# One program per engine for three stages, with weight matrices turned between the folds

## The chip, the cores and the metric

One core of a Trainium2 chip runs the whole kernel. The metric is the device time of one execution in microseconds; the runs of the kernel before took 1919.68, 1921.49 and 1924.74 us (median 1921.49). Five engines work at the same time, each on its own list of instructions: TensorE (matmul), VectorE, ScalarE, GpSimd, and SyncE, which here only issues DMAs. They meet only through semaphores, or where a block of the program ends: there all engines wait for all others.

## What is computed

A graph attention over 128 graphs of 128 nodes, 512 features, 16 heads of 32, with only the first 20 nodes of each graph as keys, and two directions of edges:

```python
row_zero = v.sum(-1) == 0
q_exp = where(row_zero[..., None], 0.0, q[:, None, :])
self_feat = concat([v, q_exp], -1) @ W_self.T + b_self
output = self_feat
for d in range(2):
    A = (adj if d == 0 else swapaxes(adj, 1, 2))[:, :, :20, :]
    cond, vb = A.sum(-1), A @ w_bias + b_bias
    kv = self_feat[:, :20]
    qh = (self_feat @ Wq[d].T + bq[d]).reshape(B, N, 16, 32)
    kh = (kv @ Wk[d].T + bk[d]).reshape(B, 20, 16, 32)
    aff = einsum('bnhd,bmhd->bnhm', qh, kh) / sqrt(32)
    w = softmax(where(cond > 0, aff, NEG) + vb, -1)
    output += einsum('bnhf,hgf->bnhg', einsum('bnhm,bmf->bnhf', w, kv), Wout[d]) + bout[d]
return v + relu(output)
```

## The kernel before

There are three stages, and each is a block of its own with one program per engine. Between two blocks all engines meet. Products with weights are made as three products of high and low parts (a number is split into a high part, written by ScalarE, and the rest, written by VectorE or GpSimd).

**Stage one, `prepare_weights`.** TensorE turns weight matrices in 128 x 128 blocks through a ring of six PSUM banks (`turn_bank`); ScalarE and VectorE copy them out. `fold(n)`, eight of them (two directions, four chunks of rows), multiplies the turned Wq with W_self into banks 6 and 7; `fold_high` on ScalarE and `fold_low` on VectorE split the result. `turn_matrix(n)` turns the four matrices Wk[0], Wk[1], Wout[0], Wout[1]; `matrix_high` and `matrix_low` split them, and the low part frees the bank. A small product gives c, the part of self_feat that comes from q (`pe_ct`); four `condition_query(pair)` products give its queries, cq. TensorE's order is: turn W_self, queries 0, folds 0 and 1, queries 1, folds 2 and 3, second half of W_self, q, folds 4 and 5, c, folds 6 and 7, matrices 0 and 1, pairs 0 and 1, matrix 2, pairs 2 and 3, matrix 3, c turned into rows (L447 to L538). The ring's banks go round in that order, pairs included. SyncE loads, and issues the first 80 KB pieces of x (`load_half_rows`, 8 DMAs for a half) after the last fold and after matrix 0; VectorE turns a half (`turn_x`), ScalarE casts it (`x_casts`), GpSimd makes its low part. SyncE ends with waits for the store of c, for all low parts of the matrices and of x.

**Stage two, `keys_and_values`.** Eight halves of 16 graphs. For each half TensorE sums the nodes' features to find zero rows (`sums`, L831), makes the 20 key nodes' features (`features`, L823), and projects them into 8 chunks of keys and 8 of values (`projection`, L823); ScalarE evacuates, VectorE turns values, and SyncE stores both to DRAM: 8 DMAs of keys and 32 of values per half (L616, L622). The last half also turns and splits the first group of x for stage three.

**Stage three, `main_loop`.** 32 groups of four graphs. In the first group: SyncE loads x's own rows xk (L1009), the edges adj0 (one DMA, L1013) and adj1 (four, L1016), waits for all stores and for `cleared`, then loads the next group's rows (L83), keys kbd (L1051) and values vbd (L1063). GpSimd first clears kbd and vbd (L1087, L1088), then makes rc, the conditions' share of each of 8 query chunks (L1116). ScalarE loads the constants wb and bb (L1307, L1308). TensorE makes the zero-row sums (L1462) into bank 4 and then `queries(c)`, c = 0 to 7 (L1482), in two banks; query c waits until query c - 2 has been evacuated by `q_evacuate` on VectorE (L1241). VectorE's order in the first group is: pick of conditions (L1154), nzb (L1234), wait for wb and bb, q_evacuate(0), weigh edges 0 (L1171, waits for adj0), q_evacuate(1), count and total of edges 0, q_evacuate(2), combine, weigh edges 1, q_evacuate(3), and so on.

Of the kernel before, what the change touches and what calls it, by code (L numbers as in the profile page):

```python
# [13 lines left out]
P = 128  # L14
Q = 32
# [75 lines left out]
def build(nc, x, cond, adj, W_self, b_self, w_bias, b_bias, Wq, bq, Wk, bk, Wout, bout, out):  # L91
# [29 lines left out]
    with ExitStack() as whole:  # L121
# [34 lines left out]
        ones = sb("ones", [P, P], F32R)  # L156

        with ExitStack() as keyed:
            sb, _ = scope(keyed)

            wkv_h = sb("wkv_h", [P, 2 * DIRS, C, F], F32R)
            wkv_l = sb("wkv_l", [P, 2 * DIRS, C, F], F32R)
            cb = sb("cb", [P, C, B + 1], F32)
            bk_s = sb("bk_s", [P, DIRS * C], F32)

            with ExitStack() as first:
                prepare_weights(nc, *scope(first), bank, locals())
            with ExitStack() as second:
                keys_and_values(nc, *scope(second), bank, locals())
        with ExitStack() as third:  # L170
            main_loop(nc, *scope(third), bank, locals())


def prepare_weights(nc, sb, sem, bank, v):
# [10 lines left out]
    qt = sb("qt", [P, C, B], F32)  # L185
# [7 lines left out]
    w1 = rows[:, 0:F // Q, :].rearrange("p (j t) k -> p j (t k)", j=R)  # L193
    w2t = nodes_t[:, :, 0:F]
    crows = cond_rows[0:B]
# [26 lines left out]
    wkv_low = sem("wkv_low")  # L222
# [4 lines left out]
    ct_out = sem("ct_out")  # L227
    cq_out = sem("cq_out")
# [3 lines left out]
    bias_done = sem("bias_done")  # L232
    stored = sem("c_stored")
    bk_done = sem("bk_done")
# [14 lines left out]
    M_TURN = [turns(C, lambda j: (wkv_low, j + 1)), turns(C, lambda j: (wkv_low, C + j + 1))]  # L249
    CQ_TURN = list(turns(2, lambda i: (cq_out, 4 * i + 4)))  # L250
    M_TURN.append(turns(C, lambda j: (wkv_low, 2 * C + j + 1)))
    CQ_TURN += turns(2, lambda i: (cq_out, 4 * i + 12))
    M_TURN.append(turns(C, lambda j: (wkv_low, 3 * C + j + 1)))
    CROW_TURN, = turns(1, lambda i: (crow_out, 1))

# [3 lines left out]
    with nc.Block() as block:  # L259
        @block.sync  # L260
        def _(sp):
            def load_natural(slot, src, loaded):
                sp.dma_start(stage[:, slot], src.rearrange("(r p) f -> p r f", p=P)).then_inc(loaded, 16)

            for r in range(R):
                sp.dma_start(w1[:, r, :], v["Wself_x"][r * P:r * P + P, :]).then_inc(w1_loaded[r], 16)
            load_natural(0, v["Wq"][0], wq_loaded[0])
            load_natural(1, v["Wq"][1], wq_loaded[1])
            sp.dma_start(cond_rows[0:B], v["cond"]).then_inc(cond_loaded, 16)
            load_natural(2, v["Wself_q"], w2_loaded)  # L270
            sp.wait_ge(pe_wq, C)
            load_natural(0, wkv[0], wkv_loaded[0])
            sp.wait_ge(pe_wq, DIRS * C)
            load_natural(1, wkv[1], wkv_loaded[1])
            sp.wait_ge(pe_w2, C)
            load_natural(2, wkv[2], wkv_loaded[2])
# [4 lines left out]
            load_half_rows(sp, v, 1, 1, kv_loaded[1])  # L281

            sp.wait_ge(crow_out, 1)
            sp.dma_start(v["c_dram"], crows).then_inc(stored, 16)
            sp.wait_ge(stored, 16)

            sp.wait_ge(wkv_low, MATS * C)
            sp.wait_ge(kv_low, 2 * C)

        @block.gpsimd  # L290
        def _(pool):
            pool.memset(identity[:], 0.0).then_inc(ident_set, 1)
            pool.memset(identity_b[:], 0.0).then_inc(ident_set, 1)
            pool.wait_ge(ident_set, 2)
            for m in (identity, identity_b):
                pool.affine_select(out=m[:], in_=m[:], compare_op=ALU.not_equal, fill=1.0, base=0,
                                   pattern=[[-1, P]], channel_multiplier=1).then_inc(ident_set, 1)

            for par in range(2):
                for j in range(C):  # L300
                    pool.wait_ge(kv_high, C * par + j + 1)
                    pool.tensor_tensor(half(nodes_l, j, par), half(nodes_t, j, par),
                                       half(nodes_h, j, par).bitcast(F32), ALU.subtract).then_inc(kv_low, 1)

        @block.vector
        def _(dve):
            def query_odd(d, j):
                dve.wait_ge(pe_wq, C * d + j + 1)
                nc.vector.tensor_copy(wqt[:, d, j, :], turn_bank(WQ_TURN[C * d + j])[:]).then_inc(wq_odd, 1)

            def fold_low(m):

                dve.wait_ge(fold_h, m + 1)
                nc.vector.tensor_tensor(wq_l[:, m // C, m % C, :], bank[6 + m % 2][:],
                                        wq_h[:, m // C, m % C, :].bitcast(F32), ALU.subtract).then_inc(fold_l, 1)

            def matrix_low(n):
                for j in range(C):
# [1251 lines left out]
```

## Time and profile before

| | us |
|---|---|
| median of the runs | 1921.49 |
| time of the profiled execution | 1921.43 |
| its span, first to last instruction | 1919.6 |
| first stage | 0 to 75.9 |
| second stage | 75.9 to 375.9 |
| third stage | 375.9 to the end |

| engine | busy us | share |
|---|---|---|
| TensorE, matmul | 1892.3 | 99% |
| VectorE | 1306.9 | 68% |
| GpSimd | 837.3 | 44% |
| ScalarE | 576.6 | 30% |

All times of the trace are counted from the span's start. PE is TensorE (PEld its weight loads, PEq its sequencer), DVE VectorE, ACT ScalarE, POOL GpSimd, SP SyncE (SPq its DMA issues). "x16" is a count of records. Of merged rows the time is from the first start to the last end. Matmuls overlap, so the distance of two starts, not the duration, is what one costs.

### The profile page before, as it was taken

What the parts mean: (1) busy time and instruction counts of PE and PEld (TensorE: products, weight loads), DVE (VectorE), ACT (ScalarE), POOL (GpSimd) and SP (SyncE); (2) the same over time, 40 slices, a digit from 0 to 9 for tenths busy, and PEclk for the clock granted to TensorE, in tenths of its full rate; (3) what the DMA queues carried; (4) which work ended last, traced back from release to release, by engine and by line L of the source; (5) the groups of instructions that cost most, each with busy time, mean ns of one, the idle gap of its engine ahead of it and who ended that gap; (6) DMA issues with size and microseconds to landing.
All of it is one profiled execution on the core that took longest, in us unless ns stands there. A gap on an engine that the chain in (4) does not pass through costs nothing.

```text
span 1919.6 us, 34533 instructions
## 1 busy us (share of the span) xinstructions
PE 1892.3 (99%) x11020; PEld 1651.3 (86%) x11020; DVE 1306.9 (68%) x1897; ACT 576.6 (30%) x1189; POOL 837.3 (44%) x746
## 2 busy tenths in 40 slices
PE   8799999999999999999999999999999999999999
PEld 6799999888888888888888888888888888888887
DVE  2433323377777777777777777777777777777776
ACT  2323323233333333333333333333333333333332
POOL 0223222254444444444444444444444444444442
PEclk9899999999999999999999999999999999999999
DMA  4222333464444444444444444444444444444431
GB/s 159 76 80 84 91 97 95 113 145 121 121 121 121 119 120 120 120 120 120 120 120 120 120 120 120 120 120 120 120 120 120 120 120 120 120 120 120 120 99 62
DMA packets 227951, 219.87 MB, mean 115 GB/s; under 512 B 58176, under 2 KB 179008, under 8 KB 223808
## 3 DMA queue, kind: packets, MB, share of 16 engines
q1 hardware_dynamic: 223440, 219.24, 41.8%
q10 hardware_dynamic: 4464, 0.02, 0.1%
q8 instruction: 27, 0.44, 0.1%
q14 instruction: 20, 0.16, 0.0%
HBM read 164.39 MB, written 54.79 MB: 114 GB/s over the span
## 4 chain that ended last, share of the span: by engine, by line
PE 78%; DVE 1%; DMA 1%; issue 0%; POOL 0%; ACT 0%; ACTq 0%; SPq 0%; DVEq 0%
PE bank L1482 36%; PE bank L1430 19%; PE bank L1418 12%; PE bank L1454 7%; PE bank L1443 4%; DMA adj<-in_mask_BxSxSx_ik 1%; PE bank L1403 0%; DVE nodes_t L88 0%; DVE qt_main L1241 0%; PE bank L1491 0%; DVE res L1228 0%; DVE sc L1205 0%; DVE res L1226 0%; DVE nodes_t L1177 0%; POOL rc L1116 0%
## 5 line engine op out<-in xcount | busy, mean ns | idle before, releaser
L1116 POOL TENSOR_TENSOR rc<-nzb,cqg 128x512 f32<-128x512 bf16 x256 | 265.4, 1042 | 412.1 <-DVE qt_main L1241 411.9
L1418 PEld LDWEIGHTS bank<-kbd,qt_main 128*128 128x128 f32 x2048 | 243.5, 192 | 19.2 <-DVE sc L1205 13.2
L1241 DVE SCALAR_TENSOR_TENSOR qt_main<-bank,bq_all,rc 128x512 f32<-128x512 f32 x256 | 189.3, 740 | 90.6 <-PE bank L1482 85.8
L1094 POOL TENSOR_TENSOR sc<-sc,mx 128x640 f32<-128x640 f32 x128 | 163.6, 1278 | 198.7 <-DVE mx L1210 198.7
L1418 PE MATMUL bank<-kbd,qt_main 128*128 128x80 f32 x2048 | 247.4, 274 | 0.3 <-DVE sc L1205 0.2
L1328 ACT ACTIVATE wtt<-bank 128x384 f32<-128x384 f32 (+1 forms) x256 | 111.4, 436 | 381.0 <-PE bank L1443 380.9
L1216 DVE TENSOR_REDUCE sm<-sc 128x32 f32<-128x640 f32 x128 | 104.6, 817 | 162.9 <-ACT sc L1320 162.9
L1482 PE MATMUL bank<-nodes_h,wq_h 128*128 128x512 f32 x512 | 210.2, 411 | 1.1 <-DVE qt_main L1241 1.1
L1482 PE MATMUL bank<-xh_odd,wq_h 128*128 128x512 f32 x512 | 210.4, 411 | 0.0
L1482 PE MATMUL bank<-nodes_h,wq_l 128*128 128x512 f32 x512 | 202.3, 395 | 0.0
L1482 PE MATMUL bank<-xh_odd,wq_l 128*128 128x512 f32 x512 | 202.0, 395 | 0.0
L1482 PE MATMUL bank<-nodes_l,wq_h 128*128 128x512 f32 x512 | 201.7, 394 | 0.0
L1482 PE MATMUL bank<-xl_odd,wq_h 128*128 128x512 f32 x512 | 201.6, 394 | 0.0
L1104 POOL TENSOR_TENSOR wt<-sc,rs 128x640 f32<-128x640 f32 x128 | 163.2, 1275 | 62.1 <-DVE rs L1219 60.5
L1454 PEld LDWEIGHTS bank<-vbd,wtt 128*128 128x128 f32 x1280 | 162.6, 191 | 11.8 <-ACT wtt L1328 1.3
L1454 PE MATMUL bank<-vbd,wtt 128*128 128x128 f32 x1280 | 163.9, 275 | 0.7 <-ACT wtt L1328 0.7
L823 PE MATMUL bank<-kv_fh,wkv_h 128*128 128x320 f32 x512 | 158.9, 310 | 2.3 <-POOL kv_fl L713 2.3
L1320 ACT ACTIVATE sc<-sc 128x640 f32<-128x640 f32 x128 | 94.5, 738 | 216.5 <-POOL sc L1094 216.5
L88 DVE STREAM_TRANSPOSE nodes_t<-rows 128x512 f32<-128x512 f32 (+1 forms) x160 | 158.0, 1016 | 1.7 <-DMA rows<-in_x 1.5
L1205 DVE TENSOR_TENSOR sc<-bank,m 128x320 f32<-128x320 f32 x256 | 111.2, 475 | 70.3 <-PE bank L1418 42.7
L823 PE MATMUL bank<-kv_fl,wkv_h 128*128 128x320 f32 x512 | 158.6, 310 | 0.0
L823 PE MATMUL bank<-kv_fh,wkv_l 128*128 128x320 f32 x512 | 158.6, 310 | 0.0
(126 smaller groups left out, 3829.6 us busy)
## 6 DMA issues: line engine op xcount, KB each, us to landing
rows<-in_x SPq DMA_DIRECT2D x128, 256.0 KB, 5.0
xk<-in_x SPq DMA_DIRECT2D x32, 1024.0 KB, 6.1
res<-c_dram SPq DMA_DIRECT2D x32, 1024.0 KB, 4.6
out<-res SPq DMA_DIRECT2D x128, 256.0 KB, 2.1
adj<-in_mask_BxSxSx_ik SPq DMA_DIRECT2D x32, 440.0 KB, 5.6
adj<-in_mask_BxSxSx_ik SPq DMA_DIRECT2D x128, 110.0 KB
k_dram<-kv_kst SPq DMA_DIRECT2D x64, 160.0 KB, 1.8
v_dram<-kv_vt SPq DMA_DIRECT2D x256, 40.0 KB
```

The costliest lines, as they stand in the source:

```text
L88: return eng.transpose(dst, src.rearrange("p t (r j) -> p t r j", j=NQ)[:, :, :, j])
L823: mm = nc.tensor.matmul(dst, a(j), b(j), start=(j == 0 and k == 0), stop=(j == C - 1 and k == 2))
L1094: pool.tensor_tensor(s, s, mx[:, b % 2, :].unsqueeze(2).to_broadcast([P, DIRS * H, NG]), ALU.subtract).then_inc(s_shifted, 1)
L1104: pool.tensor_tensor(o, e, rs[:, b % 2, :].unsqueeze(2).to_broadcast([P, DIRS * H, NG]), ALU.mult).then_inc(wt_ready, 1)
L1116: pool.tensor_tensor(rc[:, c % 2, :].rearrange("p (b n) -> p b n", b=G), nzb[:, par, :].rearrange("p (b n) -> p b n", b=G), cqg[:, par, c, ...
L1205: nc.vector.tensor_tensor(sc[:, b % 2, :].rearrange("p (h d m) -> p h d m", d=DIRS, m=NG)[:, :, d, :], s[:, 0:HM].rearrange("p (h m) -> p ...
L1241: nc.vector.scalar_tensor_tensor(out=qt[:, c, :], in0=bank[c % 2][:], scalar=bq_all[:, c:c + 1], in1=rc[:, c % 2, :], op0=ALU.add, op1=ALU ...
L1328: nc.scalar.activation(wtt[:, b % 2, lo:hi, :].rearrange("p c t -> p (c t)"), turn_bank(part, last)[:, 0:(hi - lo) * P], ACT.Copy).then_in ...
L1418: mm = nc.tensor.matmul(dst, qt[:, c, b * N:b * N + N], kbd[:, c, :, b * NG:b * NG + NG], start=True, stop=True)
L1430: mm = nc.tensor.matmul(out_bank(b, last)[:], a, m[:, j, :], start=(j == 0 and k == 0), stop=False)
L1454: mm = nc.tensor.matmul(out_bank(b, last)[:, 3 * c * DH:(3 * c + SLOTS) * DH], wtt[:, b % 2, c, :], vbd[:, c, :, b * DH:b * DH + DH], star ...
L1482: mm = nc.tensor.matmul(bank[c % 2][:], a, m, start=(j == 0 and k == 0), stop=(j == C - 1 and k == 2))
```

## The change

The three stage functions no longer open a block. Each returns five programs, one per engine, and one block at the end of `build` runs them one behind the other:

```diff
+            with nc.Block() as block:
+                @block.sync
+                def _(sp):
+                    prep[0](sp)
+                    keyed_stage[0](sp)
+                    grouped[0](sp)
...
+                @block.tensor
+                def _(pe):
+                    prep[4](pe)
+                    keyed_stage[4](pe)
+                    grouped[4](pe)
```

Where a stage relied on the meeting, a semaphore stands now:

```diff
 # stage one, SyncE
-            sp.wait_ge(stored, 16)
-
-            sp.wait_ge(wkv_low, MATS * C)
-            sp.wait_ge(kv_low, 2 * C)
 # stage two: VectorE, ScalarE, TensorE
+        dve.wait_ge(v["ct_out"], 1)
+        act.wait_ge(v["bk_done"], 1)
+        act.wait_ge(v["bias_done"], 2)
+        pe.wait_ge(v["wkv_low"], 2 * DIRS * C)
 # stage three: SyncE before the first loads of c, TensorE before and after the sums
+        sp.wait_ge(v["stored"], 16)
+        pe.wait_ge(v["cq_out"], 2 * DIRS * C)
+        pe.wait_ge(v["kv_out"], 4 * DIRS * C * v["KBLOCKS"])
```

Stage one: W_self's first half is loaded into a tile of its own and into cq instead of into the rows of x, and q turned lies in nodes_t; the rows of x are free from the start. The two condition-query banks are 6 and 7, and TensorE's order is new:

```diff
     turn_query(1)
     fold(2)
-    fold(3)
     # second half of W_self, q
-    fold(4)
-    fold(5)
+    fold(3)
     # c
-    fold(6)
-    fold(7)
-    turn_matrix(0)
-    turn_matrix(1)
+    fold(4)
+    # c turned into rows
+    turn_matrix(0)
+    fold(5)
+    turn_matrix(1)
+    fold(6)
+    turn_matrix(2)
+    fold(7)
+    turn_matrix(3)
     pe.wait_ge(small, SMALL_LOADS)
-    pe.wait_ge(ct_out, 1)
-    condition_query(0)
-    condition_query(1)
-    turn_matrix(2)
-    condition_query(2)
-    condition_query(3)
-    turn_matrix(3)
-    # c turned into rows
+    for pair in range(DIRS * C // 2):
+        condition_query(pair)
```

(lines with # stand for what is left out). ScalarE and VectorE follow:

```diff
 # VectorE, after fold_low(2), W_self's second half and the biases
+        fold_low(3)
+        fold_low(4)
         matrix_low(0)
         dve.wait_ge(pe_ct, 1)
         turn_x(0)
+        fold_low(5)
+        matrix_low(1)
+        turn_x(1)
+        fold_low(6)
         matrix_low(2)
+        fold_low(7)
         matrix_low(3)
+        condition_queries(range(DIRS * C))
 # ScalarE, after c
+        fold_high(4)
+        act.wait_ge(pe_crow, 1)
+        nc.scalar.activation(crows, turn_bank(CROW_TURN)[0:B, :], ACT.Copy).then_inc(crow_out, 1)
         matrix_high(0)
+        fold_high(5)
         x_casts(0)
+        matrix_high(1)
+        fold_high(6)
+        x_casts(1)
         matrix_high(2)
+        fold_high(7)
         matrix_high(3)
```

SyncE loads x half 0 right behind matrix 0, x half 1 right behind matrix 2, then stores c, and loads matrix 3 last:

```diff
     sp.wait_ge(pe_wq, C)
     load_natural(0, wkv[0], wkv_loaded[0])
+    load_half_rows(sp, v, 0, 0, kv_loaded[0])
     sp.wait_ge(pe_wq, DIRS * C)
     load_natural(1, wkv[1], wkv_loaded[1])
     sp.wait_ge(pe_w2, C)
     load_natural(2, wkv[2], wkv_loaded[2])
-    sp.wait_ge(pe_fold, DIRS * C)
-    load_half_rows(sp, v, 0, 0, kv_loaded[0])
-    sp.wait_ge(pe_wkv, C)
-    load_natural(0, wkv[3], wkv_loaded[3])
     load_half_rows(sp, v, 1, 1, kv_loaded[1])
     sp.wait_ge(crow_out, 1)
     sp.dma_start(v["c_dram"], crows).then_inc(stored, 16)
+    sp.wait_ge(pe_wkv, C)
+    load_natural(0, wkv[3], wkv_loaded[3])
```

Stage two: the clearing of vst on VectorE comes after the first features instead of first, the pick of the condition after the zero flags. Stage three: GpSimd clears kbd and vbd in the first group after two rc products, and first waits there for all stores of keys and values; the zero-row sums go to bank 6 instead of bank 4.

```diff
+        def clear():
+            for s in v["k_stored"]:
+                pool.wait_ge(s, 16 * DIRS * C * v["KBLOCKS"])
+            for s in v["v_stored"]:
+                pool.wait_ge(s, 32 * DIRS * C * v["KBLOCKS"])
+            pool.memset(kbd[:], 0.0).then_inc(cleared, 1)
+            pool.memset(vbd[:], 0.0).then_inc(cleared, 1)
...
+                if c == 2:
+                    if not first:
                         normalise(g - 1, G - 1)
+                    else:
+                        clear()
```

## Rows read from the trace of the kernel before

**Rows 1.** The page, busy us, share of the span and instructions of each engine.
```profile
PE 1892.3 (99%) x11020; PEld 1651.3 (86%) x11020; DVE 1306.9 (68%) x1897; ACT 576.6 (30%) x1189; POOL 837.3 (44%) x746
```

**Rows 2.** What TensorE waited for: us in total, times, longest.
```profile
PE bank L1462 <- PEq L601: 3.2, 1, 3.2
PE bank L823 <- POOL kv_fl L713: 2.3, 1, 2.3
```

**Rows 3.** Stretches: us, busy us of each engine, granted clock, DMA share, GB/s.
```profile
61.73:67.05 5.32, 5.32 (x33) 5.32 (x33) 3.57 (x12) 1.90 (x4) 1.43 (x2) 0.68 0.60 102
75.89:79.20 3.31, 3.31 (x12) 3.31 (x13) 1.48 (x3) 0.00 (x0) 0.16 (x1) 0.50 0.26 75
89.70:92.90 3.20, 3.20 (x14) 3.20 (x14) 0.00 (x0) 0.53 (x1) 0.00 (x0) 0.50 0.15 51
377.00:379.50 2.50, 2.50 (x8) 1.91 (x7) 2.50 (x2) 0.00 (x0) 2.50 (x2) 0.50 0.48 118
384.90:386.00 1.10, 0.25 (x2) 0.08 (x1) 0.75 (x1) 1.04 (x5) 0.06 (x1) 1.00 0.98 137
```

**Rows 4.** TensorE in time, first stage: start us, us, work, count, [idle before].
```profile
43.67 7.15 PE L470 MATMUL bank<-wqt,rows 128*128 128x512 f32 x16
...
54.15 3.78 PE L480 MATMUL bank<-cb,wqt 128*128 128x129 f32 x32
57.77 1.91 PE L447 MATMUL bank<-identity,stage 128*128 128x128 f32 x16
61.73 5.48 PE L480 MATMUL bank<-cb,wqt 128*128 128x129 f32 x32 [2.06 <-DVE bq_all L334]
...
75.89 0.60 PE L831 MATMUL bank<-nodes_h,ones 128*128 128x320 f32 x1 [6.50 <-PEq L259]
...
80.07 0.31 PE L823 MATMUL bank<-nodes_h,ws_h 128*128 128x320 f32 x1
...
85.64 0.30 PE L823 MATMUL bank<-nodes_h,ws_l 128*128 128x320 f32 x1
```

**Rows 5.** ScalarE and VectorE in time, first stage.
```profile
61.59 2.04 ACT L396 ACTIVATE wkv_h<-bank 128x512 fp32r<-128x512 f32 x4
...
62.20 2.48 DVE L320 TENSOR_TENSOR wkv_l<-bank,wkv_h 128x512 fp32r<-128x512 f32 x4
...
70.72 2.65 DVE L88 STREAM_TRANSPOSE nodes_t<-rows 128x320 f32<-128x320 f32 x4
```

**Rows 6.** The chain that ended last: start us, us, what.
```profile
376.32 10.38 DMA adj<-in_mask_BxSxSx_ik
```

**Rows 7.** SyncE's issues in time, from 355 us.
```profile
362.48 12.89 SPq L622 DMA_DIRECT2D v_dram<-kv_vt  x32
...
376.32 0.50 SPq L1013 DMA_DIRECT2D adj<-in_mask_BxSxSx_ik  x1
...
380.44 3.23 SPq L83 DMA_DIRECT2D rows<-in_x  x4
383.71 6.85 SPq L1051 DMA_DIRECT2D kbd<-k_dram  x4
```

**Rows 8.** VectorE and TensorE in time, first group.
```profile
386.73 1.19 DVE L1171 TENSOR_TENSOR prod<-adj,wb 128x880 f32<-128x880 int32 x1 [0.86 <-DMA adj<-in_mask_BxSxSx_ik]
387.84 0.74 DVE L1241 SCALAR_TENSOR_TENSOR qt_main<-bank,bq_all,rc 128x512 f32<-128x512 f32 x1
...
394.66 0.50 PE L1482 MATMUL bank<-nodes_h,wq_h 128*128 128x512 f32 x1 [0.20 <-DVE qt_main L1241]
```

**Rows 9.** DMA issues of the whole span: count, KB each, median us to landing.
```profile
adj<-in_mask_BxSxSx_ik SPq DMA_DIRECT2D x32, 440.0 KB, 5.6
...
bb<-in_L_cond_b_bias ACTq DMA_DIRECT2D x1, 0.5 KB, 8.8
```

**Rows 10.** GpSimd in time, second boundary.
```profile
378.04 2.23 POOL L1088 MEMSET vbd<- 128x2560 f32 x1
```

**Rows 11.** Tile kbd: duration ns min/median/max, first and last start us; landing.
```profile
L1051 SPq DMA_DIRECT2D kbd<-k_dram x128: 316/317/4854, 383.7 to 1862.0; - x128
...
DMA to landing us min/median/max: 2.3/5.5/9.8
```

More of the change, by code:

```diff
@@ L248, in prepare_weights @@
     CT_TURN, = turns(1, lambda i: (ct_out, 1))
[L249 to L253, printed above, removed]
     CROW_TURN, = turns(1, lambda i: (crow_out, 1))
+    M_TURN = [turns(C, lambda j, n=n: (wkv_low, C * n + j + 1)) for n in range(MATS)]
@@ L538 @@
+    return sync_program, vector_program, gpsimd_program, scalar_program, tensor_program
 SMALL_LOADS = 16 * 5
@@ new lines, in sync_program, with one_half @@
+    def sync_program(sp):
+        def one_half(blk, n, par, first, last, tail):
+            if not tail:
+                sp.wait_ge(x_turned, C * (n + 1))
+                load_half_rows(sp, v, n + 2, par, loaded[par])
+            elif not last:
+                sp.wait_ge(x_turned, C * HALVES)
+                load_group_rows(sp, v, 0, main_loaded)
+            for p in range(NK):
+                sp.wait_ge(kv_out, 2 * NK * n + p + 1)
+                sp.dma_start(v["k_dram"][p, :, bass.ds(n * HB, HB), :],
+                             kst[:, p % 2, :].rearrange("p (b m) -> p b m", m=NG)).then_inc(k_stored[p % 2], 16)
+            for m in range(NK):
+                d, c = m // C, m % C
+                sp.wait_ge(v_turned, NK * n + m + 1)
+                for k in range(NQ):
+                    sp.dma_start(v["v_dram"][NQ * c + k, d, :, bass.ds(n * HB, HB), :],
+                                 vt[Q * k:Q * k + NG, m % 4]).then_inc(v_stored[m % 4], 16)
+        halves(sp, one_half)
@@ L1075, in _ @@
-            groups(sp, group)
-            sp.wait_ge(out_stored, 64 * GROUPS)
-        @block.gpsimd
-        def _(pool):
-            def low(g, par, chunks=range(C)):
-                for j in chunks:
-                    pool.wait_ge(x_high, C * g + j + 1)
-                    pool.tensor_tensor(xl[par][:, j, :], xt[:, j, :], xh[par][:, j, :].bitcast(F32),
-                                       ALU.subtract).then_inc(x_low, 1)
+                pool.wait_ge(s, 32 * DIRS * C * v["KBLOCKS"])
@@ new lines, in group @@
+        def group(g, par, i, first, last):
+            pool.wait_ge(cqg_ready, g + 1)
+            pool.wait_ge(nzb_ready, g + 1)
+            for c in range(NC):
+                if c == 2:
+                    if not first:
+                        normalise(g - 1, G - 1)
+                    else:
+                        clear()
+                if due(NC * g + max(c - 1, 0)):
+                    pool.wait_ge(q_out, NC * g + max(c - 1, 0))
+                pool.tensor_tensor(rc[:, c % 2, :].rearrange("p (b n) -> p b n", b=G),
+                                   nzb[:, par, :].rearrange("p (b n) -> p b n", b=G),
+                                   cqg[:, par, c, :].unsqueeze(2).to_broadcast([P, G, N]),
+                                   ALU.mult).then_inc(rc_ready, 1)
+            if not last:
+                if due(G * g):
+                    pool.wait_ge(pe_self, G * g)
+                low(g + 1, 1 - par, range(0, 3))
+            shift(g, 0)
+            shift(g, 1)
+            normalise(g, 0)
+            normalise(g, 1)
+            shift(g, 2)
+            if not last:
+                low(g + 1, 1 - par, range(3, C))
+            normalise(g, 2)
+            shift(g, 3)
+            if last:
+                normalise(g, 3)
```

1771 lines of the change are left out of this document (864 added, 907 removed).

## The prediction, made before the changed kernel ran

> **What bounds the kernel now.** I read the page's busy shares first: TensorE is busy 99% of the span [rows 1], so time can only come from its idle stretches and from stretches at the lower clock. The list of what TensorE waited for and its timeline name them: 3.2 us and 6.50 us "for PEq", which are the two meetings of all engines, 2.3 us for a low part of the features, 2.06 us for a copy of condition queries [rows 2, 4]. Then the granted clock: behind these waits stretches run at 0.50, that is 1.2 instead of 2.4 GHz, or at a mix (0.68) [rows 3]. All these lie before 395 us; behind, the busy share leaves nothing at stake. Last I read the chain of waits: its longest piece is not TensorE but 10.38 us of the first edge transfer, right behind the second meeting [rows 6].
>
> All of the sum is made against the profiled execution: span 1919.6, its own time 1921.43 us, 0.06 below the median 1921.49 of the runs shown.
>
> **First stage.** Edits: folds 3 to 7 now alternate with turned matrices; condition queries get banks 6 and 7 and go last; x halves are loaded early; c goes out early. TensorE's work stays the same (8 folds, 4 matrices, 4 pairs, the two small transposes), so I slide it together. Up to fold 2 nothing changes. Before, the stage's last work ends at 75.89 - 6.50 = 69.39. What goes:
> - the 2.06 us wait at 61.73 [rows 4];
> - the slow stretch behind it: the last two pairs take 67.05 - 61.73 = 5.32 us at a mean clock of 0.68 [rows 3, 4], the first two 57.77 - 54.15 = 3.62 us, so 1.70;
> - the wait from 69.39 to 75.89, 6.50 us [rows 4]. In it x half 1 was loaded, turned, cast and its low parts made; all that now lies beside folds.
> So the sums of stage two can start at 75.89 - 2.06 - 1.70 - 6.50 = 65.6 us.
> - The 56 matmuls of sums and first features ran from 75.89 to 85.79 (last start 85.64 and 0.15 of pitch), 9.90 us, the first 3.3 us of it at 0.50 [rows 3, 4]. With TensorE busy until they start I take them at the full pitch of 0.147 (39 rows from 80.07 to 85.64, 5.57 us for 38 steps): 8.21 us, so 1.69 less.
> Sum: 2.06 + 1.70 + 6.50 + 1.69 = 11.95 us.
>
> Does anything new wait? With folds of 3.50 us (7.15 for two, less the tail), matrices of 1.8 and pairs of 1.81, the new order runs, counted back from 65.6: fold 4 to 40.2, transposes of c to 40.7, matrix 0 to 42.5, fold 5 to 46.0, matrix 1 to 47.8, fold 6 to 51.3, matrix 2 to 53.1, fold 7 to 56.6, matrix 3 to 58.4, pairs to 65.6. ScalarE needs 0.51 per copy (2.04 for four), VectorE 0.62 (2.48 for four) and 2.7 us to turn a half (2.65, four) [rows 5]. The third block of matrix 2 (52.2) needs the bank of matrix 1's first block: ScalarE splits fold 5 (46.6) and casts x half 0 (four copies, 48.6) ahead of it, high part 49.1, low part 49.8: 2.4 us to spare. Matrix 3's third block (57.5) needs matrix 2's first: VectorE turns half 1 from 51.1 to 53.8, ScalarE casts to 54.3, high and low parts to 55.5: 2.0 to spare. The third pair (62.0) needs the first pair out of bank 6: VectorE has matrix 3's low parts until 60.3, then four small copies, 60.9: 1.1 to spare. These margins are the cover; if one fails, a wait comes back. On SP's queue each x half is 8 DMAs, 6.5 us at the 0.81 of one in row 380.44 [rows 7]: the first half goes behind matrix 0 and ahead of matrix 1, wanted at 46.0, the second behind matrix 2; both are issued before 37, since the wait ahead of the second is for the turned W_self's other half, at 29.2. The store of c waits for its copy at 41.4, and matrix 3, behind it, is issued at 42.5 and wanted at 56.6. Nothing there is near.
>
> The 2.32 us wait for the last feature's low part [rows 2] is a chain of VectorE, ScalarE and GpSimd; it stays, and so does the slow stretch behind it (0.50 from 89.7 to 92.9 [rows 3]); were that to go, its 3.2 us at half clock would give 1.6 more. The clearing of vst (under 1 us) and the pick of the condition move on VectorE to places where TensorE has features to do: nothing.
>
> **Second boundary.** This is where I don't give the kernel what it seems to offer. In the time of before, TensorE's last projection ends at 372.73. Without the meeting the sums (1.83 us) start at once and queries 0 and 1 (2.75 each) end at 380.05. But VectorE evacuates query 0, then multiplies edges 0 (row 386.73, begun when they landed), then evacuates query 1 (387.84), and query 3 waits for that [rows 8]. Edges 0 are issued by SP behind x's own rows, and SP is not held by the meeting but by its own queue: 32 stores of values from 362.48 for 12.89 us, to 375.37 [rows 7]. So the edges go out at 375.9 instead of 376.32, 0.45 sooner, and land 0.45 sooner if the landing time stays 10.38 [rows 6, 7]: at 386.25. Query 1 is out at 388.15, query 3 starts there, 0.45 sooner. TensorE waits in all 388.15 - 380.05 - 2.75 = 5.35 us in place of 3.2 and 0.85 (row 384.90 [rows 3]). Next in line: before, query 5 started at 394.66, released by VectorE's copy of query 3 [rows 8]; VectorE works through from 386.73 to there, so it could release it at 394.2 now. TensorE needs from 388.15 two queries, 5.5 us, to 393.65, if the clock is full. After a wait of over 2 us the clock fell each time [rows 3], and the stretch that ran slow cost 1.7 us (the first term above, and 1.69 again). With it query 5 starts at 395.35, 0.7 us later than before. I take this: before, the slow stretch lay ahead of the edges and cost nothing; now it lies behind them. So -0.7 us, with -2.4 (two falls) and +4.3 as ends. The +4.3: edges land 5.6 us after issue, as they do later in the kernel [rows 9], at 381.5; then VectorE is the bound: the constant bb (8.8 us to landing [rows 9], issued by ScalarE about 0.9 us behind the last projection, at 373.6) lets the first evacuation go at 382.4 at the latest, and the 7.9 us from 386.73 to 394.6 lead to 390.4.
>
> The DMA rule of the Trainium skill bears on which end is nearer (DMA: Bandwidth & Descriptors, section Queues, rings and completion order): each DMA engine takes the descriptors of one queue's ring in their order. By it the edges stay behind the 1 MB of x that SP issued before them and group rows issued behind them don't slow them, so 10.38 stays and the sum is as above; by the other reading their landing shortens, since the group rows now go out later, and the sum moves towards rival B's 1905.2. No row here decides it.
>
> **The clearing of kbd and vbd** (2.23 us each [rows 10]) moves behind two rc products and the last stores. These had landed by 380.3, when the second clearing ended and SP went on, at 380.44 [rows 7, 10], so it ends between 382.1 and 384.7. rc of query 2 follows by 385.8, wanted at 390. SP is queued behind it: 4 loads of group rows (3.23 us), 4 of kbd (6.85) [rows 7], so kbd is issued by 394.9 and landed by 401 with a landing of some 6 us; scores want it at 404. Hidden, at nothing; vbd has longer.
>
> Sum: 11.95 - 0.7 = 11.25; 1921.43 - 11.25 = 1910.2 us.
>
> **Rivals.**
> A, the clock does not fall at the second boundary. For it: the 0.85 us wait before 386 left the clock at 1.00 [rows 3]; against: the waits of 2.06 us and more did not. Then +0.45 in place of -0.7: 1909.0.
> B, the edges land much sooner, since no group rows go out beside them. For it: 5.6 us later in the kernel [rows 9]; against: there they don't follow 1 MB directly. 11.95 + 4.3: 1905.2.
> C, first stage gives part back: one of the margins of 1.1 to 2.4 us fails, since ScalarE now holds turned matrices behind folds and x casts. A wait like the 2.06 us one and its slow stretch of 1.70 return: 1914.0.
> D, slower than before: SP's queue behind the clearing makes the first scores wait for kbd. It decides from a landing at 404.5 + 11.95 = 416.5 in the time of before. The longest issue of a kbd DMA was 4.85 us and the longest landing 9.8 [rows 11]: 384.7 + 3.23 + 4 x 4.85 + 9.8 = 417.1; with the slow stretch the kernel ends at 1921.43 + 0.6 + 1.7 = 1923.7. Against it: the issue times all had to be the worst one.
> That the change doesn't do what it says is in part in the forecast: the second meeting goes, yet the edges hold the same place.
>
> **How the numbers follow.** Forecast 0.50, A 0.18, B 0.12, C 0.15, D 0.04, and 0.01 for anything else on the slow side. The range from 1906.0 to 1914.0 holds forecast, A, C and the half of B in which edges are only partly sooner; with two falls the forecast is 1911.9, inside. Within 0.3% (5.8 us, about what a measurement of this kernel can tell from no change) lies only the tail of C: 0.05. Faster 0.90, slower 0.05.
>
> **What would show it.** In the changed kernel: stage-two sums start at 65.6 us with a granted clock of 1.00, and no wait for condition queries; a 2.3 us wait before the first projection at about 76; the last projection ends near 360.8; SP issues x and edges some 3 us after it; then the longest wait of TensorE, 5 us in one or two pieces, for VectorE's copy of query 1 behind the edges, a clock of 0.50 behind it, and query 5 at 383.4. Wrong would be: a wait for wkv_l or cq in the first stage (C), a first wait behind the boundary under 2 us (B), scores waiting for kbd (D), or a slow stretch in the first 65 us.

## The result, and the profile after

| | us |
|---|---|
| before, median of 6 runs beside it | 1923.03 (1919.68 to 1924.74) |
| changed kernel, median of 6 runs | 1907.59 (1906.23 to 1908.99) |
| ratio of the two | 0.9922, 95% interval 0.9909 to 0.9935 |
| profiled execution, before and after | 1921.43 and 1906.23 |
| their spans | 1919.6 and 1904.4 |

The profiled executions differ by 15.2 us; the forecast took 11.25 from that same execution. So the time lies inside the range, and the change is worth a third more than I gave it. The median, 1907.59, is near the range's lower end of 1906.0, which I had put there for half of rival B; to lie inside the range was in part luck.

The page's busy shares of the changed kernel, to be read against [rows 1]:

```profile
PE 1887.3 (99%) x11020; PEld 1646.9 (86%) x11020; DVE 1303.7 (68%) x1897; ACT 575.5 (30%) x1189; POOL 836.6 (44%) x746
```

TensorE has the same 11020 matmuls and 5 us less busy time: part of the gain is a better clock, not only shorter waits. What TensorE waited for (us in total, times, longest):

```profile
PE bank L849 <- POOL kv_fl L739: 2.7, 1, 2.7
...
PE bank L1517 <- DVE qt_main L1276: 1.9, 2, 1.7
```

No "PEq" is left: both meetings of [rows 2, 4] are gone. The one for kv_fl grew from 2.3 to 2.7, and a new one for the copies of queries stands at the second boundary. (A longer wait of 3.7 to 3.8 us, for the first load of W_self, stands at the start of both kernels.) TensorE in time (start, us, work, [idle before]):

```profile
58.80 7.31 PE L510 MATMUL bank<-cb,wqt 128*128 128x129 f32 x64
65.87 0.39 PE L857 MATMUL bank<-nodes_h,ones 128*128 128x320 f32 x1
...
74.02 0.30 PE L849 MATMUL bank<-nodes_h,ws_l 128*128 128x320 f32 x1
77.04 0.64 PE L849 MATMUL bank<-kv_fh,wkv_h 128*128 128x320 f32 x1 [2.72 <-POOL kv_fl L739]
```

All four pairs of condition queries run in 7.31 us without a wait, and the sums of stage two start right behind them, 10.02 us earlier than in [rows 4]. Stretches of the changed kernel (us, busy us of each engine, granted clock, DMA share, GB/s):

```profile
58.80:66.00 7.20, 7.20 (x67) 7.20 (x66) 3.93 (x16) 1.01 (x3) 0.00 (x0) 1.00 0.01 1
65.87:74.30 8.43, 8.43 (x59) 8.19 (x57) 3.71 (x9) 1.42 (x3) 5.08 (x7) 1.00 0.01 2
77.04:80.40 3.36, 3.36 (x14) 3.36 (x15) 0.00 (x0) 0.00 (x0) 0.00 (x0) 0.56 0.00 0
...
368.00:374.00 6.00, 4.32 (x19) 3.24 (x18) 2.74 (x4) 2.89 (x8) 4.33 (x4) 1.00 0.99 241
```

Against [rows 3] the slow stretches at the condition queries and at the sums are gone, the one behind the kv_fl wait remains (0.56), and the second boundary is at 1.00 throughout. SyncE's issues there:

```profile
351.05 12.90 SPq L650 DMA_DIRECT2D v_dram<-kv_vt  x32
364.00 0.41 SPq L1036 DMA_DIRECT2D xk<-in_x  x1
364.45 0.51 SPq L1040 DMA_DIRECT2D adj<-in_mask_BxSxSx_ik  x1
...
370.57 1.92 SPq L83 DMA_DIRECT2D rows<-in_x  x4
372.53 3.92 SPq L1079 DMA_DIRECT2D kbd<-k_dram  x4
```

As in [rows 7] the edges go out behind 32 stores, now 3.15 us after TensorE's last projection. But they don't take 10.38 us to land. The DMA issues of 355 to 380 us in the changed kernel (count, KB each, median us to landing):

```profile
adj<-in_mask_BxSxSx_ik SPq DMA_DIRECT2D x1, 440.0 KB, 6.8
...
wb<-in_L_cond_w_bias ACTq DMA_DIRECT2D x1, 5.5 KB, 2.3
bb<-in_L_cond_b_bias ACTq DMA_DIRECT2D x1, 0.5 KB, 2.6
```

The same view of the kernel before, 365 to 385 us:

```profile
adj<-in_mask_BxSxSx_ik SPq DMA_DIRECT2D x1, 440.0 KB, 10.4
...
wb<-in_L_cond_w_bias ACTq DMA_DIRECT2D x1, 5.5 KB, 5.8
bb<-in_L_cond_b_bias ACTq DMA_DIRECT2D x1, 0.5 KB, 8.8
```

3.6 us less for the same 440 KB. The constants land sooner too, and that matters by itself: VectorE's copy of query 0 needs bb. In the kernel before it waited for it, and TensorE's 0.85 us wait for that copy is a wait for bb:

```profile
385.11 0.75 DVE L1241 SCALAR_TENSOR_TENSOR qt_main<-bank,bq_all,rc 128x512 f32<-128x512 f32 x1 [4.80 <-DMA bb<-in_L_cond_b_bias]
```

VectorE and TensorE in the first group of the changed kernel, against [rows 8]:

```profile
371.26 1.09 DVE L1206 TENSOR_TENSOR prod<-adj,wb 128x880 f32<-128x880 int32 x1 [4.52 <-DMA adj<-in_mask_BxSxSx_ik]
...
373.07 0.50 PE L1517 MATMUL bank<-nodes_h,wq_h 128*128 128x512 f32 x1 [1.68 <-DVE qt_main L1276]
```

Here VectorE waits 4.52 us for the edges, and TensorE 1.68 us for the copy of query 1 behind them.

For the ledger I use four marks, in every kernel: P, the first projection's start; E, the last projection's end (start of its last matmul and 0.31; values to 0.01 by rounding); K, the first scores (product of kbd and qt_main); and the span.

| | P | E | K | span | P to E | E to K | K to end |
|---|---|---|---|---|---|---|---|
| before | 88.26 | 372.72 | 404.52 | 1919.6 | 284.46 | 31.80 | 1515.1 |
| changed | 77.04 | 361.30 | 388.96 | 1904.4 | 284.26 | 27.66 | 1515.4 |
| gain | 11.22 | | | 15.2 | 0.20 | 4.14 | -0.4 |

### The profile page after: what moved, and what is told of

It reads as the page before. It is cut to its first block, busy times and chain, and to the rows that moved or that the text cites. A ratio compares the mean times of both kernels' runs of the same rounds, so it can differ in the third digit from the quotient of the medians.

```text
span 1904.4 us, 34516 instructions
## 1 busy us (share of the span) xinstructions
PE 1887.3 (99%) x11020; PEld 1646.9 (86%) x11020; DVE 1303.7 (68%) x1897; ACT 575.5 (30%) x1189; POOL 836.6 (44%) x746
## 4 chain that ended last, share of the span: by engine, by line
PE 95%; DVE 1%; DMA 0%; issue 0%; SPq 0%; POOL 0%; ACT 0%; ACTq 0%; DVEq 0%
PE bank L1517 37%; PE bank L1463 19%; PE bank L849 14%; PE bank L1451 12%; PE bank L1487 8%; PE bank L1476 4%; PE bank L857 0%; PE bank L1436 0%; DMA adj<-in_mask_BxSxSx_ik 0%; PE bank L1526 0%; DVE nodes_t L88 0%; DVE qt_main L1276 0%; SPq L650 0%; DVE nodes_t L1212 0%; POOL rc L1152 0%
```

## The experiments

My theory after the result: the first stage did what I said, and the surplus is the edges' landing. It was slow before because ScalarE's two loads of constants (wb and bb, one small packet per partition) went out at the same moment as xk and the edges, and their packets took turns with the big ones on the DMA engines. Without the meeting ScalarE issues them at 361.35, 2.65 us ahead of xk, and both have landed by 364.4, when the edges go out. The rival (theory two, the reason my rival B gave): the edges land sooner because the group rows no longer go out right behind them. The packets of the kernel before from 378 to 380 us speak for the first (queue: packets, MB, share of 16 engines; q1 carries SyncE's loads, q10 the small ones):

```profile
q1 hardware_dynamic: 110, 0.23, 47.1%
q10 hardware_dynamic: 82, 0.00, 2.1%
```

Three small packets for every four large ones, and 114 GB/s in all. The changed kernel moved this from 366 to 370 us, at 366 GB/s:

```profile
q1 hardware_dynamic: 986, 1.46, 105.9%
```

The small packets' own time is only 2.1% there, and the engines stand idle for half of the stretch. So "taking turns" is my reading of how the small ones hold the large ones; the runs below show that they do, not how.

The unmodified kernel beside the first four runs below: median 1922.73 us (16 runs); beside the next four 1921.09 (7 runs).

| | median us (runs) | ratio, 95% | P | E | K | span |
|---|---|---|---|---|---|---|
| three_blocks | 1914.26 (4) | 0.9954, 0.9937 to 0.9970 | 80.30 | 365.03 | 396.43 | 1912.2 |
| old_stage_one | 1914.03 (7) | 0.9960, 0.9948 to 0.9971 | 83.63 | 368.09 | 395.81 | 1911.3 |
| constants_late | 1909.34 (4) | 0.9927, 0.9911 to 0.9944 | 76.95 | 362.66 | 395.06 | 1909.7 |
| before_constants_early | 1925.86 (10) | 1.0018, 1.0008 to 1.0028 | 91.72 | 374.54 | 405.85 | 1923.6 |
| rows_early | 1906.48 (2) | 0.9920, 0.9900 to 0.9940 | 77.17 | 360.11 | 389.26 | 1904.2 |
| vst_later | 1905.53 (4) | 0.9917, 0.9901 to 0.9934 | 76.87 | 359.81 | 387.46 | 1902.3 |
| edges_first | 1903.83 (4) | 0.9905, 0.9889 to 0.9922 | 77.15 | 362.79 | 387.97 | 1902.6 |
| features_between | 1902.56 (4) | 0.9899, 0.9883 to 0.9916 | 75.47 | 358.37 | 386.13 | 1901.0 |
| both_better | 1897.73 (4) | 0.9871, 0.9855 to 0.9888 | 74.80 | 357.70 | 382.88 | 1896.6 |

The stretch from K to the end has the same work in every kernel, and its time goes from 1513.7 to 1515.8 us (1517.8 in before_constants_early). I have no cause for these differences, so of a span only what shows up to K is explained.

What TensorE pays from E to K can be added up. Where it waits for nothing (edges_first, both_better) it takes 25.18 us. To that come its waits and half of the time that it then works at a clock of 0.50 (us):

| | waits, and for what | at 0.50 | 25.18 + waits + half | measured |
|---|---|---|---|---|
| before | 3.19 meeting, 0.85 and 0.20 copies | 3.41 | 31.13 | 31.80 |
| changed | 1.68 and 0.24 copies | 0 | 27.10 | 27.66 |
| three_blocks | 3.34 meeting | 5.76 | 31.40 | 31.40 |
| constants_late | 4.25 copy of query 0 | 5.86 | 32.36 | 32.40 |
| before_constants_early | 3.19 meeting | 5.86 | 31.30 | 31.31 |
| rows_early | 2.11 copy | 3.42 | 29.00 | 29.15 |

**three_blocks: the meetings put back.** The new stage one, but each stage a block of its own.

```diff
-            with nc.Block() as block:
-                @block.sync
-                def _(sp):
-                    prep[0](sp)
-                    keyed_stage[0](sp)
-                    grouped[0](sp)
+            for part in (prep, keyed_stage, grouped):
+                with nc.Block() as block:
+                    @block.sync
+                    def _(sp):
+                        part[0](sp)
...
```

> The changed kernel with its three programs per engine in three blocks again, so both meetings of all engines are back; the new order of the first stage stays. The first meeting should cost some 1.5 us (VectorE's last query copies end at 66.7 us, TensorE's pairs at 66.0), stage-two sums at 67 to 68 us. At the second meeting theory one (the small packets of the constants wb and bb, on ScalarE's queue, take turns with those of xk and the edges and slow them) expects edges 0 to land about 10 us after issue again and a span of about 1910. Theory two (the next group's rows, issued 4 us behind the edges before the change, slowed them) expects 6.8 us, since GpSimd's clearing still comes late and holds the rows back, and a span of about 1906.5.

TensorE in time at the two meetings, and the edges in the DMA issues:

```profile
69.14 0.38 PE L848 MATMUL bank<-nodes_h,ones 128*128 128x320 f32 x1 [1.16 <-PEq L177]
...
368.37 0.77 PE L1487 MATMUL bank<-nodes_h,ones 128*128 128x512 f32 x1 [3.34 <-PEq L177]
```

```profile
adj<-in_mask_BxSxSx_ik SPq DMA_DIRECT2D x1, 440.0 KB, 9.8
```

SyncE issued the group rows only at 379.55, behind the edges' landing, and yet the landing is 9.8: that refutes theory two. ScalarE's wb went out at 368.18, beside xk at 368.17. E to K is 31.40, as before. A meeting whose last work is TensorE's own makes it wait 1.16 us at the first boundary. At the second the 31.40 - 27.66 = 3.7 more are the meeting's wait and the slow clock behind it; TensorE waited for no copy, so the late landing cost it nothing here. P is 3.3 later: 0.3 by a later start of the turned Wq, 1.55 because the first fold ran slow in this execution (below), and the remaining 1.4 by the meeting.

**old_stage_one: no meetings, but the old order in stage one.** Folds 0 to 7, matrices 0 and 1, pairs, matrix 2, pairs, matrix 3; SyncE's, ScalarE's and VectorE's lists to match.

```diff
-    fold(4)
-    # c turned into rows
-    turn_matrix(0)
-    fold(5)
-    turn_matrix(1)
-    fold(6)
-    turn_matrix(2)
+    fold(6)
     fold(7)
-    turn_matrix(3)
+    turn_matrix(0)
+    turn_matrix(1)
+    condition_query(0)
+    condition_query(1)
+    turn_matrix(2)
+    condition_query(2)
+    condition_query(3)
+    turn_matrix(3)
+    # c turned into rows
...
```

> One block as in the changed kernel, but the first stage's order of folds, matrices, pairs, copies and x loads as before. This tells how much of the 11.4 us ahead of the last projection the order brought and how much the missing meeting alone. Expected: the wait of about 2 us for query copies and its slow stretch are back, sums start at about 71 us (held by the low part of matrix 3) in place of 65.9, and VectorE's turning of x half 1 ahead of the zero flags makes the first projection later still, at about 83 in place of 77.0; the span is 1910 to 1911. If the meeting alone had cost the time, the first projection would be at 78 to 79. The second boundary should look as in the changed kernel under both theories: edges landing about 6.8 us after issue.

The waits come back, shared out otherwise (us in total, times, longest):

```profile
PE bank L851 <- POOL kv_fl L741: 3.6, 1, 3.6
PE bank L510 <- DVE bq_all L361: 2.3, 1, 2.3
...
PE bank L859 <- DVE wkv_l L347: 1.5, 1, 1.5
```

P is 6.6 us later than in the changed kernel, E to K (27.7) the same. So of the gain up to P, 6.6 is the order of stage one and 4.6 the meeting's absence alone. The split holds only in this sequence: taken the other way, three_blocks gives 1.4 to the meeting's absence and the rest to the order, since each hides part of what the other costs.

**constants_late: the constants back beside xk.** The decisive run for the landing: one wait ahead of ScalarE's two loads, nothing else.

```diff
+        act.wait_ge(nzb_ready, 1)
         act.dma_start(wb[:], ...partition_broadcast(P)).then_inc(edge_consts, 16)
         act.dma_start(bb[:], ...partition_broadcast(P)).then_inc(edge_consts, 16)
```

> The changed kernel, but ScalarE waits for the zero flags nzb before it issues the constants wb and bb, so they go out at about 364 us, beside xk, as before the change. Theory one (small packets of the constants slow xk and the edges): xk lands about 8 us after issue in place of 5.6, edges about 10 in place of 6.8, query 3 waits some 3.5 us longer, the span is about 1908 and the slow clock may come on top (1909.7). Theory two (group rows slowed the edges): xk 5.6 and edges 6.8 stay, the span stays at 1904.4 within half a us.

DMA issues, then VectorE's copy of query 0 and TensorE's wait for it, then the stretch behind that wait:

```profile
adj<-in_mask_BxSxSx_ik SPq DMA_DIRECT2D x1, 440.0 KB, 10.5
...
wb<-in_L_cond_w_bias ACTq DMA_DIRECT2D x1, 5.5 KB, 4.9
bb<-in_L_cond_b_bias ACTq DMA_DIRECT2D x1, 0.5 KB, 7.7
```

```profile
373.45 0.75 DVE L1276 SCALAR_TENSOR_TENSOR qt_main<-bank,bq_all,rc 128x512 f32<-128x512 f32 x1 [8.21 <-DMA bb<-in_L_cond_b_bias]
...
374.25 0.79 PE L1518 MATMUL bank<-nodes_h,wq_h 128*128 128x512 f32 x1 [4.25 <-DVE qt_main L1276]
```

```profile
374.20:380.00 5.80, 5.75 (x14) 4.49 (x15) 3.62 (x5) 1.93 (x6) 2.08 (x2) 0.50 1.17 159
```

6 KB on another queue make 440 KB land 3.7 us later. E to K is 32.40 instead of 27.66, a 4.7 us cost: 2.3 more waiting and 2.9 for the clock at 0.50, less the 0.5 that the sum above leaves open in the changed kernel. But the wait is not the one I expected. It is query 2's, for the copy of query 0, and that copy waited for bb itself, 7.7 us from issue to landing. The edges landed only at 376.3, when TensorE was already working through query 2 at the low clock, and it waited for nothing more. So this run shows what the constants do to the edges' landing, but not what that landing costs TensorE; what it costs here is bb's own. The total agrees with my forecast for this boundary (31.80 + 0.7 = 32.5), by another wait and so by chance. The Trainium skill says that loads issued by different engines run on the same 16 DMA engines and interleave (DMA: Bandwidth & Descriptors, section Issuing engines are not separate DMA queues); the rows agree, and they add the price: 3.7 us.

**before_constants_early: the kernel before, constants loaded at its start.**

```diff
 # stage one, ScalarE, ahead of its first wait; taken out of stage three
+            act.dma_start(v["wb"][:], v["w_bias"].partition_broadcast(P)).then_inc(v["edge_consts"], 16)
+            act.dma_start(v["bb"][:], v["b_bias"].partition_broadcast(P)).then_inc(v["edge_consts"], 16)
```

> The kernel before the change, but wb and bb are loaded at the start of the first stage. Theory one: edges 0 land 6.8 us after issue in place of 10.4; TensorE then becomes the bound up to query 5, which starts about 1.5 us sooner, and the span is about 1918. Theory two: edges 10.4 as before, only the 0.85 us wait for query 0's copy goes and comes back at query 3; the span stays 1919.6.

```profile
adj<-in_mask_BxSxSx_ik SPq DMA_DIRECT2D x1, 440.0 KB, 7.0
```

The landing is cured in the old kernel too (7.0 for 10.4), with the group rows where they were, so this too speaks against theory two. But E to K is only 0.5 shorter: the waits for copies are gone, 1.05 us, while TensorE worked 5.86 us at 0.50 behind the meeting instead of 3.41. And the time went up by 3.1 us. P is 3.5 later: ScalarE is held by issuing the two loads (3.3 and 0.7 us), behind five others, and makes its first copy of W_self at 13.48 instead of 8.44; the turned Wq waits 2.3 us for its load instead of 1.5, two further waits of 1.1 follow, and the first folds take 9.02 us instead of 7.23, their first matmuls at the low clock (below). Another 2.7 us lie behind K (1517.8 instead of 1515.1), for which I have no cause.

**rows_early: group rows right behind the edges.** Theory two's own test.

```diff
         load_kept(0, 0)
         load_edges(0)
+        sp.wait_ge(x_turned, C)
+        load_group_rows(sp, v, 1, xs_loaded)
```

> The changed kernel, but SyncE issues the next group's rows (4 x 256 KB) right behind the edges instead of behind the clearing of kbd and vbd, some 4 us sooner, so they stand 2 to 4 us behind edges 0 as before the change or closer. If later transfers on the same queue slowed the edges (theory two), they land some 2 to 3 us later than 6.8 us after issue. If a queue's transfers keep their order and only the constants' packets did it (theory one), the landing stays 6.8 to 7.0 us and query 3 waits 1.7 us as before.

```profile
adj<-in_mask_BxSxSx_ik SPq DMA_DIRECT2D x1, 440.0 KB, 7.2
```

0.4 us at most, in two runs. E to K grew by 1.5: a wait of 2.1 us at query 3 instead of 1.7, and a mean clock of 0.72 over 371 to 377 instead of 1.00. Theory two is refuted from both sides.

**vst_later: the clearing of vst behind the last low part.** In the changed kernel VectorE clears 128 x 1024 numbers just when GpSimd makes the low part that TensorE waits for. GpSimd, then VectorE:

```profile
75.72 1.26 POOL L739 TENSOR_TENSOR kv_fl<-kv_fs,kv_fh 128x320 fp32r<-128x320 f32 x1 [0.86 <-ACT kv_fh L770]
```

```profile
75.28 0.91 DVE L720 MEMSET kv_vst<- 128x1024 f32 x1
```

```diff
+        dve.wait_ge(f_low, C)
         nc.vector.memset(vst[:], 0.0).then_inc(pads_set, 1)
```

> The changed kernel, but VectorE clears vst only after the last low part of the first features. In the changed kernel the clearing (75.28 to 76.19 us) stands beside GpSimd's last low part, which took 1.26 us in place of 0.86, and TensorE waited 2.72 us in place of 2.32. Theory: the clearing made GpSimd slower; the low part goes back to 0.86 us and the wait to 2.3 us, 0.4 us in all. Rival: GpSimd's time is its own scatter and the wait stays at 2.7. The whole time moves by less than the measurement can tell; a slow clock stretch behind the wait that is longer or shorter by 3.4 us can move the span by 1.7 us either way.

```profile
75.95 0.86 POOL L740 TENSOR_TENSOR kv_fl<-kv_fs,kv_fh 128x320 fp32r<-128x320 f32 x1 [0.85 <-ACT kv_fh L771]
```

The low part is back at 0.86, and TensorE's wait at 2.32. The memset cost 0.40 us although it touches another tile and runs on another engine. The low part took 1.25 to 1.26 us in all six executions where the memset ran beside it, and 0.86 to 0.89 in the five where it did not. (A small copy of 0.17 us, cond's, runs right behind the memset and moved with it, so its share isn't told apart.) The Trainium skill has VectorE and GpSimd share one pair of ports that one instruction holds whole while the other is blocked, but it names only VectorE instructions in a 2-port mode or with two inputs in SBUF (SBUF — State Buffer, section SBUF: two separate sides). A memset has no input, and no row tells its mode. Were it such a holder, GpSimd would be held up to 76.19, 0.47 us after its start, near the measured 0.40; by the rule for the others nothing would have been lost, and the measurement decides. Of the 2.1 us of shorter span only 0.17 show at P, since the turned Wq started 0.25 later here; 1.3 are the clock between P and E, which is the next point, and 0.6 lie behind K.

**edges_first: edges issued ahead of x's own rows.**

```diff
-        load_kept(0, 0)
         load_edges(0)
+        load_kept(0, 0)
```

> The changed kernel, but SyncE issues edges 0 and 1 ahead of xk. If the 1 MB of xk in front of the edges is what they wait for, edges 0 land some 4 us after issue, at about 368, before VectorE wants them at 366.7 or just behind; query 3 no longer waits (1.68 us) and the span falls by 1.7 to 1.9 us to about 1902.6. The row sums that need xk come 3 us later and have until 390. Rival: the landing is bounded by something else (stores of values still under way) and stays near 6.8: no change.

```profile
adj<-in_mask_BxSxSx_ik SPq DMA_DIRECT2D x1, 440.0 KB, 3.6
```

E to K is 25.18, 2.5 less: TensorE waits for no copy any more, so in the changed kernel the edges' landing did hold it. 1.4 of it went on a longer slow stretch at the first projection, and 0.8 came behind K; that the span is the expected 1902.6 to a tenth is chance. Two executions whose code is the same up to there, vst_later (first) and edges_first (second), 77 to 83.5 us:

```profile
77.00:83.50 6.50, 6.50 (x45) 6.50 (x46) 1.48 (x3) 1.06 (x2) 1.01 (x2) 1.00 0.15 52
```

```profile
77.00:83.50 6.50, 6.35 (x25) 6.35 (x26) 0.00 (x0) 0.53 (x1) 0.10 (x1) 0.52 0.07 25
```

(Up to there but for the 0.40 us of the memset.) P to E is 282.8 to 282.9 where nothing runs slow (vst_later, rows_early, features_between, both_better, before_constants_early), 284.3 to 284.7 in four executions and 285.6 to 285.7 in two; rows_early and edges_first have the same 2.72 us wait and end on opposite sides.

The mean granted clock of every run tells more than these single executions; one stretch of 3.4 us at 0.50 turns 1.000 into 0.999. It reads 1.000 in none of the 12 runs of the three kernels with the 2.72 us wait (changed, rows_early, edges_first), in 3 of the 4 of vst_later with 2.32, and in 7 of the 8 of the two kernels below without a wait there. It doesn't say where in the run the slow stretch lies.

**features_between: two pairs of condition queries behind the first features.** They fill TensorE's wait for the low part.

```diff
-        for pair in range(DIRS * C // 2):
+        for pair in range(2):
             condition_query(pair)
+        LATE["pairs"] = lambda: [condition_query(pair) for pair in (2, 3)]
...
 # stage two, TensorE behind the first half's features
+        LATE["pairs"]()
```

> The changed kernel, but stage two's first sums and features run between the second and third pair of condition queries, so that two pairs (3.6 us) cover the chain to the last low part (2.7 us); tiles of the stages are laid out anew for it. Expected: no wait at the first projection and no slow stretch behind it; it starts at about 74.2 us in place of 77.04, and the 3.4 us at half clock go, 1.7 us; span 1904.4 - 2.8 - 1.7 = 1899.9. Rival: the clock falls on its own whatever TensorE does, and only 2.8 us come.

```profile
75.47 0.39 PE L854 MATMUL bank<-kv_fh,wkv_h 128*128 128x320 f32 x1
```

No wait before the first projection, and no slow stretch behind it. One execution can't exclude that the stretch stayed away by itself, as in rows_early; the run clocks above make it unlikely. P came 1.6 us sooner than in the changed kernel, and would have been at 73.8 but for the first fold, which ran slow here as in three_blocks and before_constants_early. The same four matmuls in three executions, the changed kernel, three_blocks, features_between:

```profile
15.49 2.08 PE L495 MATMUL bank<-wqt,w_low 128*128 128x512 f32 x4 [0.87 <-DVE wqt L335]
```

```profile
15.81 3.62 PE L486 MATMUL bank<-wqt,w_low 128*128 128x512 f32 x4 [0.88 <-DVE wqt L326]
```

```profile
15.24 3.71 PE L496 MATMUL bank<-wqt,w_low 128*128 128x512 f32 x4 [0.88 <-DVE wqt L335]
```

The view's clock column reads 1.00 for all three, but that is what it prints where the trace has no record of the clock. The first record, at 1.00, begins at 18.76 us in features_between, 19.14 in three_blocks and 21.78 in before_constants_early, and between 14.5 and 15.3 in the other eight executions, ahead of the first fold. Matmuls start 0.85 us apart up to that moment and 0.43 behind it: so I read it as the first fold running at 1.2 GHz there until the clock's first rise.

**both_better: the last two edits together.**

> The changed kernel with both edits that were measured alone: the first two pairs of condition queries ahead of the features and the other two behind the first folds (features_between), and the edges' copy issued ahead of the inputs' (edges_first). If the two gains lie in different places of the chain they add: of the changed kernel's span 1904.4 the run features_between took 3.4 us and the run edges_first 1.8 us, the latter with a slow stretch of some 3 us more behind the first projection than the changed kernel had, which has no cause once that projection no longer waits. Sum 1904.4 - 3.4 - 1.8 = 1899.2, and down to 1896 where the slow stretch was lost in it; time about 1900 to 1901. Edges land in 3.6 us, no wait of TensorE for qt_main, clock 1.00 from the first sums to the first scores. Rival: the end is set elsewhere (by VectorE's prod and the copies of the queries), and the edges' early landing gives nothing once the clock stays up: span 1901.0 as features_between alone.

Two stretches, the first projections and the whole second boundary:

```profile
74.80:84.00 9.20, 9.20 (x66) 9.20 (x65) 2.82 (x8) 1.59 (x3) 3.08 (x4) 1.00 0.15 54
358.00:386.00 28.00, 28.00 (x132) 23.07 (x130) 22.57 (x29) 5.73 (x14) 16.45 (x13) 1.00 0.95 211
```

Up to K the gains add, and the slow stretch is lost as well: span 1896.6, 7.8 under the changed kernel (2.2 at P, 1.4 from P to E, 2.5 from E to K, and 1.7 behind K, for which there is no cause). TensorE is busy and at full clock through both boundaries. It beats both kernels: 1897.73 us against 1921.93 of the kernel before beside it, a ratio of 0.9871 whose interval lies clear of the changed kernel's 0.9922.

## Why the prediction was right in sign and range, and short in size

- **2.06, 1.70 and 6.50 us (condition queries, their slow stretch, the first meeting's wait): right.** Sum 10.26; the sums started 10.02 sooner. The missing 0.2 is the start of the kernel: the turned Wq began at 10.94 instead of 10.58, for its load. None of the margins of 1.1 to 2.4 us failed, so rival C is out.
- **1.69 (slow stretch of the sums): right.** First sum to last feature: 9.75 before, 8.15 after, 1.60.
- **vst's clearing "nothing": wrong by 0.40**, shown by vst_later. I asked what TensorE had to do then, not what GpSimd did, whose result TensorE was about to wait for.
- **The slow stretch behind that wait "stays": right.** It is there in the trace, and all six runs have a mean clock of 0.999, one such stretch's worth. But it isn't tied to the wait alone: behind the same 2.72 us rows_early has none, and edges_first 6 us.
- **Second boundary, -0.7: this step failed.** It said "SP is held by its own queue, so the edges go out 0.45 sooner"; they did (3.15 us behind E instead of 3.60). It went on "and land 0.45 sooner if the landing time stays 10.38", and that did not hold: 6.8. constants_late gives back 10.5 by one wait in ScalarE's list. So TensorE waited 1.92 us in all where I had 5.35, and the clock, for whose fall I had put 1.7, stayed up. I had both pieces in hand: 8.8 us for half a KB [rows 9], and in the sum itself bb issued 0.9 us behind the last projection, ahead of xk. I used the 8.8 only as a bound of rival B and never asked what made so small a load take so long, and whether it did the same to its neighbours. The term is 4.14 instead of -0.7. Against the kernel before it consists of 2.3 less waiting (the table above: 1.92 for 4.24) and 1.7 for the clock, 0.1 left over. In the kernel before, the late edges themselves cost TensorE at most the 0.20; their 10.4 would have counted only once the meeting was gone.
- **The clock there:** with the edges early TensorE waited 1.68 us instead of 5, and the clock stayed at 1.00. Where the wait was 4.3 us (constants_late) it fell to 0.50 over 374.2 to 380, as the step had it.
- **Clearing of kbd and vbd behind the stores, hidden: right.** GpSimd's last clearing ended at 370.41; SyncE issued the rows at 370.57 and kbd from 372.53, landing in 6.2 us, against scores at 388.96. Rival D is out.
- **Rivals:** B came nearest in time (1905.2), for a reason that rows_early, three_blocks and before_constants_early refute. (Its term was also too large: the 7.9 us from row 386.73 on start behind the first copy, 0.7 us after 382.4, so B was worth 3.6, not 4.3.) The Trainium skill's ring order, which I cited with the forecast (DMA: Bandwidth & Descriptors, section Queues, rings and completion order), holds as far as it goes: edges_first, with the order turned round, lands them in 3.6. It was no ground for 10.38, since another queue's packets came in between.

The ledger: first stage and first features 11.42 gained where 11.95 was forecast, second boundary 4.14 for -0.7, and 0.4 lost behind K; together 15.2.

## What to carry to other kernels

When a meeting of all engines goes, don't only slide TensorE's work: list every DMA of every engine that the meeting had lined up at one moment, and see which now goes out alone. A tiny load that is broadcast to 128 partitions is worth moving as much as a large one; a landing of 8.8 us for 0.5 KB is a sign that it shares the way with something, and both pay: the large load lands later, and whoever needs the tiny one waits for it (4.25 us of TensorE in constants_late). A landing alone isn't a cost, though; ask which wait of the bounding engine ends last. And a wait of TensorE of 2 to 3 us is worth filling twice over, once for itself and once for the slow stretch that may follow.

## What was not expected of the hardware

- Two loads of 6 KB in all, one small packet per partition each, cost 440 KB behind them 3.0 to 3.7 us: 9.8 to 10.5 us to landing when issued beside xk (before, three_blocks, constants_late), 6.8 to 7.0 otherwise (changed, old_stage_one, before_constants_early). In those three TensorE lost at most 0.20 us by the late edges, since another wait (the meeting, or bb) had come first.
- A wait of 2.3 to 2.7 us was followed by 0 to some 6 us of TensorE at 1.2 GHz, behind the same 2.72 us too, worth 0 to 2.8 us from P to E.
- Behind a wait of 0.88 us the first four matmuls of the first fold took 2.08 us in some executions and 3.6 to 3.7 in others. The slow ones ran at half pace until the trace's first record of the clock, which begins at 18.8 to 21.8 us there instead of 14.5 to 15.3: by that they ran at 1.2 GHz. Why the rise came later is open.
- Where a VectorE memset of 0.91 us (and the small copy behind it) overlapped a GpSimd instruction of 0.86 us, that took 0.40 longer.
